# Row-centred output weights and a reordered way from cross attention into latent attention

## The chip, the cores and the metric

One core of one Trainium2 chip. The metric is the device time of one execution in microseconds (us), the median over runs; lower is better. Times of single instructions come from the profile of one execution.

## What is computed

One transformer layer over 256 rows of 512 channels. It has three parts, and each adds to the residual stream `x`: cross attention onto a context of 4096 rows (16 heads of 32), latent attention (MLA, 16 heads), and a mixture of experts. The change lies at the end of the first part and the beginning of the second:

```python
# cross attention, its end
ctx = softmax(q @ k.T / sqrt(32) + mask) @ v      # 16 heads
delta = rs * (ctx @ Wo.T + bo)                    # rs: residual scale, 0 to 0.3
mu, var = delta.mean(-1), delta.var(-1)
x = x + (delta - mu) / sqrt(var + 1e-5) * ln_gamma + ln_beta
# latent attention, its beginning
h = layernorm(x)
cq  = rms_norm(h @ w_qa.T, q_a_ln_w)              # 384 latents
ckv = h @ w_kva.T                                 # 128 latents and 64 rotary
q, kv = cq @ w_qb.T, rms_norm(ckv[:128]) @ w_kvb.T
x = x + causal_attention(q, kv, rotary) @ w_o.T
```

## The kernel before

TensorE is fed with float16 pairs: a float32 value times a scale is split into a high and a low half, by ScalarE (the high half) and then VectorE (the rest), and three products stand for one. All matmuls are issued by one helper, at L1184, so the rows below carry that line for nearly all of them.

**Cross attention** runs over 8 blocks of 512 context rows (`x_block`). A block has 8 steps `i`, the code's pairs of score tiles. In step `i` TensorE computes the scores of that step, then weighs the values with the probabilities of the step before (`weigh`), and in blocks 0 to 6 projects one of 8 units of keys or values of the next block into the one bank `pP` (`project`, which waits until ScalarE has emptied that bank of the unit before). ScalarE in each step first empties the bank (`evac`, L472 and L473 for keys) and then takes the exponents of two tiles (L540); VectorE clips them (L867) and adds them up (L879). The program of every engine is a fixed list, so whatever stands behind a wait on an engine waits too. Block 7 has no projection: there the chain from scores to exponents to the next scores sets the pace, and small work is put into its steps: on ScalarE the bias `bo` in float16 (L555, L556, step 0) and the latent weights' high halves (L558, steps 0 to 3); on VectorE the scales (`prep_scales`, L807 to L811, step 0), `x + beta` (`prep_rows`, L817, step 1), the low halves (L892, steps 2 and 3), and in steps 4 and 6 the sums of the probabilities (L897) and their reciprocals (L899), which TensorE spreads over the rows of each head in the next step.

The output weights `woT` (1 MB) lie in the place of a context buffer. SyncE's list issues their load at L349, behind the wait of block 6 for its first exponent and the load of a mask (L290):

```python
            x_block(NBLK - 2, 0, load=False)     # wait exp_done(16 * 6 + 1), load_mask(7)
            sp.wait_ge(s["ctx_lo"], 4 * (NBLK - 1))
            sp.dma_start(woT, a["woT"]).then_inc(s["wo_in"], 16)
```

In the kernel before the first to wait for `wo_in` is TensorE, in step 6 of block 7.

**The end of cross attention.** After the last `weigh`, VectorE takes the last sums and a reciprocal per 128 rows (L910, L913); TensorE spreads it by a matmul (`spread_den`), ScalarE copies it out (L574), VectorE multiplies (L851) and adds the value bias (L855), and TensorE multiplies with `woT` (`out_rows`). Then, per half `t` of the rows: mean and variance (L924, L925), the scaled variance (L926), a power by GpSimd (L448), the residual row (L930), the mean taken off (L933), four transposes (L1386), the high halves on ScalarE (L578), the squares (L580) and the low halves on VectorE (L938).

**Into latent attention.** `latents(t, low)` are the first projections, `turn_latents` (L1405) transposes their normed result, and `first_q` and `first_kv` project the queries, keys and values of head pair 0. ScalarE and VectorE then split them: rotary queries (L994, L626, L999), queries (L621, L1003), keys (L630, L1008), values (L635); then the scores of the pair start. `residual(t)` puts `x1_sb` times a scale into the banks of the output by a float32 matmul with `ident_s`, in pair 0. The output of each pair is added in these banks, first in pair 1 (`out_product`).

Of the kernel before, what the change touches and what calls it, by code (L numbers as in the profile page):

```python
# [61 lines left out]
def build(nc, a, out):  # L62
# [4 lines left out]
    with ctx:  # L67
# [34 lines left out]
        rs2 = sb("rs2", [128, 1])  # L102
# [7 lines left out]
        ident_s = sb("ident_s", [128, 128])  # L110
# [19 lines left out]
        def take(n, dt=f32):  # L130
# [133 lines left out]
            den_read rows_done den_ready denb_done rden_ready ctxn_ready delta_done  # L264
# [132 lines left out]
        def _(pool):  # L397
# [14 lines left out]
            pool.memset(ident_s[:, :], 0.0).then_inc(s["pch"], 1)  # L412
            pool.memset(onerow[:, :], 0.0).then_inc(s["pch"], 1)
            pool.memset(bo16, 0.0).then_inc(s["pch"], 1)
            chain[0] = 9
# [6 lines left out]
            for r in (0, 32):  # L422
# [17 lines left out]
                                    pattern=[[-1, 128]], channel_multiplier=1))  # L440
            link(pool.affine_select(out=ident_s[:, :], in_=ident_s[:, :], compare_op=ALU.not_equal, fill=SH * SW, base=0,
# [16 lines left out]
        def _(act):  # L458
# [63 lines left out]
            def x_block(b, p, proj=True, split=True, last=False):  # L522
                first = isinstance(b, int) and b == 0
                for i in range(PAIRS_X):
# [23 lines left out]
                    if b == NBLK - 2 and i == HC:  # L548
                        split_q(0, 0)
                        split_kv(0, 0)  # L550
                    if last and i < HC:
                        if i == 0:
                            act.wait_ge(s["const_ready"], 1)
                            act.wait_ge(s["row_in"], 64)
                            act.activation(bo16[0:1, :], bo_b[0:1, :], ACT.Copy, scale=SW)  # L555
                            act.activation(bo_t[32:33, :], bo_b[32:33, :], ACT.Copy, scale=SW).then_inc(s["bo_hi"], 1)  # L556
                            act.wait_ge(s["lat_in"], 16)
# [14 lines left out]
            for t in range(TT):  # L572
                act.wait_ge(s["denb_done"], t + 3)
                act.activation(rden[:, 3, 128 * t:128 * t + 128], pS[:, t, 0:128], ACT.Copy).then_inc(s["rden_ready"], 1)  # L574
# [71 lines left out]
            hi_latents(1)  # L646
            rope_hi(0, 0)
            mla_evac_q(0, 0, 2)
            mla_evac_k(0, 0)
# [6 lines left out]
            with act.Fori(0, PAIRS - 5, 2) as m:  # L656
                mla_pair(m, 0)
                mla_pair(m + 1, 1)
# [76 lines left out]
        def _(dve):  # L735
# [66 lines left out]
            def prep_scales():  # L802
# [5 lines left out]
                dve.tensor_tensor(rs2[:, :], rs[:, :], rs[:, :], ALU.mult)  # L808
                dve.tensor_scalar(gam_b[:, :], gam_b[:, :], rs[:, 0:1], None, ALU.mult)
                dve.wait_ge(s["bo_hi"], 1)  # L810
# [36 lines left out]
            def context(gs, cols, k):  # L847

                dve.wait_ge(s["rden_ready"], k)
                for g in gs:  # L850
                    last = dve.tensor_tensor(ctxn[:, g, cols], pO[:, g // 2, T * (g % 2):T * (g % 2) + T][:, cols],  # L851
# [330 lines left out]
        def _(pe):  # L1182
# [353 lines left out]
            def mla_pair(m, p, proj=True, before=True):  # L1536
# [10 lines left out]
                if not before:  # L1547
                    residual(0)
# [213 lines left out]
```

## Time and profile before

| | |
|---|---|
| median of 3 runs | 729.77 us (729.39 to 730.04) |
| the profiled execution | 731.32 us, its span 729.6 us |
| mean granted clock of TensorE | 0.998 |
| TensorE matmuls | 710.9 us busy, 97% |
| VectorE | 611.0 us, 84% |
| ScalarE | 435.0 us, 60% |
| GpSimd | 11.3 us, 2% |

In the span, cross attention takes until about 322 us, latent attention until about 434 us, the experts the rest. PE is TensorE's matmul part, PEld its weight loads, DVE is VectorE, ACT is ScalarE, POOL is GpSimd, SP is SyncE. The span runs from the first to the last instruction. A row of the timeline has the start, the time, the engine, the line, the operation, what it writes and reads, how many were merged, and in brackets how long the engine was idle before it and for what.

### The profile page before, as it was taken

The numbers are of one execution on the slowest core, as the hardware profiler recorded it, in microseconds if no ns is written. First come the engines' busy times: TensorE is split into PE (matmuls) and PEld (weight loads), VectorE is DVE, ScalarE is ACT, GpSimd is POOL, SyncE is SP. The second block draws the span as 40 slices with busy tenths as digits, with TensorE's granted clock in tenths as the row PEclk, the third lists the DMA queues.
The fourth block names the chain that finished last, engine by engine and source line by source line (L and its number), as shares of the span: only waits on it lengthen the run. The fifth ranks groups of instructions, "written<-read, shape, count | busy, mean of one in ns | idle before, by whom it ended". The sixth has DMA issues, their size and how long they took to land.

```text
span 729.6 us, 16489 instructions
## 1 busy us (share of the span) xinstructions
PE 710.9 (97%) x6716; PEld 441.3 (60%) x6716; DVE 611.0 (84%) x942; ACT 435.0 (60%) x597; POOL 11.3 (2%) x36
## 2 busy tenths in 40 slices
PE   8999999999999999888999989999999999999998
PEld 3544444444444444445777758777777777777775
DVE  4778999999999998776888986788888888888885
ACT  4677777777777787834668844444444444444442
POOL 3000000000000000001000000000000000000000
PEclk9999999999999999999999999999999999999999
DMA  8560101010100010014242512577777777777770
GB/s 316 176 264 1 60 2 60 1 60 2 59 3 1 12 49 1 4 47 174 77 134 92 191 44 64 175 240 238 224 243 228 234 242 245 217 242 237 227 243 33
DMA packets 29864, 94.17 MB, mean 129 GB/s; under 512 B 5824, under 2 KB 15088, under 8 KB 28400
## 3 DMA queue, kind: packets, MB, share of 16 engines
q1 hardware_dynamic: 28944, 92.31, 38.6%
q10 hardware_dynamic: 864, 1.07, 0.5%
q8 instruction: 41, 0.67, 0.4%
q14 instruction: 15, 0.12, 0.1%
HBM read 92.76 MB, written 0.57 MB: 128 GB/s over the span
## 4 chain that ended last, share of the span: by engine, by line
PE 90%; DVE 3%; ACT 3%; DMA 2%; issue 1%; SPq 0%; POOL 0%; ACTq 0%; DVEq 0%
PE pS L1184 39%; PE pP L1184 29%; PE pO L1184 13%; PE pD L1184 9%; DMA arena<-in_wkT 1%; DMA mask_i<-in_mask 1%; ACT arena L540 1%; PE pO L1552 1%; DVE arena L781 0%; DVE arena L899 0%; DVE xn L1102 0%; ACT arena L593 0%; SPq L312 0%; ACT arena L578 0%; PE pS L1386 0%
## 5 line engine op out<-in xcount | busy, mean ns | idle before, releaser
L1184 PE MATMUL pS<-arena 128*128 128x256 f16 (+3 forms) x2185 | 254.2, 273 | 1.9 <-ACT arena L578 0.8
L1184 PEld LDWEIGHTS pS<-arena 128*128 128x128 f16 (+1 forms) x2185 | 213.5, 101 | 46.2 <-issue 2.1
L1184 PE MATMUL pP<-arena 128*128 128x512 f16 x980 | 239.4, 382 | 0.6 <-ACT arena L460 0.6
L1184 PEld LDWEIGHTS pP<-arena 128*128 128x128 f16 x980 | 91.9, 99 | 124.5 <-issue 12.2
L540 ACT ACTIVATE arena<-pS,mblk 128x1024 f32<-128x1024 f32 x128 | 147.3, 1205 | 8.8 <-PE pS L1184 8.8
L1013 DVE SCALAR_TENSOR_TENSOR arena<-arena 128x1536 f16<-128x1536 f32 x72 | 126.1, 1752 | 0.8 <-ACT arena L654 0.8
L694 ACT ACTIVATE arena<-pS 128x256 f32<-128x256 f32 x72 | 27.6, 383 | 154.2 <-PE pS L1184 154.2
L1184 PE MATMUL pO<-arena 128*32 128x256 f32 (+7 forms) x1370 | 108.6, 359 | 1.9 <-DVE arena L1008 1.9
L654 ACT ACTIVATE arena<-arena 128x1536 f16<-128x1536 f32 x72 | 106.4, 1477 | 1.0 <-PE pP L1184 1.0
L867 DVE TENSOR_SCALAR arena<-arena 128x1024 f32<-128x1024 f32 x128 | 87.1, 691 | 17.6 <-ACT arena L540 14.8
L1184 PE MATMUL pD<-arena 128*128 128x512 f16 x288 | 77.9, 379 | 0.0
L1184 PEld LDWEIGHTS pO<-arena 128*32 128x32 f32 (+3 forms) x1370 | 48.8, 107 | 38.2 <-issue 17.4
L1146 DVE TENSOR_TENSOR arena<-pS,arena 128x256 f32<-128x256 f32 x72 | 30.6, 425 | 36.0 <-ACT arena L694 36.0
L1184 PE MATMUL pS<-work,arena 32*128 32x256 f16 x1536 | 53.4, 269 | 4.0 <-ACT arena L540 4.0
L1184 PEld LDWEIGHTS pS<-work,arena 32*128 32x128 f16 x1536 | 33.7, 93 | 33.5 <-issue 24.5
L1184 PEld LDWEIGHTS pD<-arena 128*128 128x128 f16 x288 | 28.2, 98 | 17.3 <-DVE arena L1158 0.2
L472 ACT ACTIVATE arena<-pP,xb 128x512 f16<-128x512 f32 x29 | 19.9, 687 | 30.9 <-PE pP L1184 30.9
L1154 DVE TENSOR_TENSOR arena<-arena 128x256 f32<-128x256 f32 x68 | 28.9, 426 | 7.7 <-DVE arena L1146 1.1
L879 DVE TENSOR_TENSOR x_sb<-x_sb,arena 128x1024 f32<-128x1024 f32 x26 | 31.8, 1222 | 1.7 <-DVE x_sb L879 0.5
L879 DVE TENSOR_TENSOR xn<-xn,arena 128x1024 f32<-128x1024 f32 x26 | 31.8, 1222 | 1.7 <-DVE xn L879 0.5
L879 DVE TENSOR_TENSOR xT<-xT,arena 128x1024 f32<-128x1024 f32 x26 | 31.8, 1222 | 1.4
L879 DVE TENSOR_TENSOR arena<-arena 128x1024 f32<-128x1024 f32 x26 | 31.8, 1222 | 1.4
(252 smaller groups left out, 493.5 us busy)
## 6 DMA issues: line engine op xcount, KB each, us to landing
arena<-in_units SPq DMA_DIRECT2D x72, 768.0 KB, 4.9
arena<-w_scratch SPq DMA_DIRECT2D x136, 64.0 KB, 2.7
arena<-in_ctxT SPq DMA_DIRECT2D x7, 1024.0 KB, 4.9
mw_in<-in_mla_in SPq DMA_DIRECT2D x8, 832.0 KB, 6.7
mw_out<-in_mla_out SPq DMA_DIRECT2D x8, 512.0 KB, 3.7
wlatT<-in_wlatT SPq DMA_DIRECT2D x1, 1280.0 KB, 10.6
arena<-in_ctxT ACTq DMA_DIRECT2D x4, 256.0 KB, 6.5
arena<-in_wkT SPq DMA_DIRECT2D x4, 256.0 KB, 5.6
```

What stands on the lines that cost most here:

```text
L472: act.activation(kh[:, p, n], bank, ACT.Identity, bias=xb[:, 1, n:n + 1], scale=1.0 / SW)
L540: act.activation(probs[:, tile], step_scores(st), ACT.Exp, bias=mblk[:, p, 1, tile:tile + 1], scale=mblk[:, p, 0, tile:tile + 1])\
L654: act.activation(uwh[:, slot], uw32[:, slot], ACT.Copy, scale=SW).then_inc(s["unit_hi"], 1)
L694: act.activation(sg[:, buf], pS[:, bank, 0:T], ACT.Silu, scale=1.0 / (SA * SW)).then_inc(s["silu_ready"], 1)
L867: dve.tensor_scalar(probs[:, t], probs[:, t], LO, HI, ALU.max, ALU.min).then_inc(s["clip_done"], 1)
L879: dve.tensor_tensor(acc, acc, probs[:, t], ALU.add).then_inc(s["sum_done"], 1)
L1013: dve.scalar_tensor_tensor(uwl[:, slot], uw32[:, slot], SW, uwh[:, slot], ALU.mult, ALU.subtract).then_inc(s["unit_lo"], 1)
L1146: dve.tensor_tensor(m1[:, buf], pS[:, bank, T:2 * T], sg[:, slot], ALU.mult).then_inc(s["m1_ready"], 1)
L1154: dve.tensor_tensor(m2[:, buf], m1[:, buf], weight, ALU.mult).then_inc(s["m2_ready"], 1)
L1184: return pe.matmul(o, lhsT, rhs, start=start, stop=stop, **kw)
L1552: last = pe.transpose(pO[:, j, 128 * i:128 * i + 128], pm[:, j, 128 * i:128 * i + 128], ident[:, :])
```

## The change

- **Centred weights.** The mean over the output channels is taken off `woT` and `bo`, so that `delta` has a mean of zero. ScalarE sums the four chunks of `woT` with an in-place copy in block 6, steps 0, 5, 6 and 7; VectorE makes means and subtracts in block 7, step 0. The bias in float16 moves to step 1 of block 7 and waits for the centred weights, `prep_rows` moves from step 1 to step 4, ahead of the sums there.
- **Variance.** `bn_stats` and `bn_aggr` are replaced by a square with an accumulator on ScalarE.
- **Last sums.** Head group 3 is summed with a matrix of ones into columns 256 to 511 of `pD`, so that every row of a head holds the sum and nothing has to be spread. VectorE multiplies, ScalarE adds the value bias; group 3 comes ahead of group 2.
- **TensorE filled.** Two and three matmuls of zeros (`keep_warm`) around the transposes of the first rows.
- **First projections.** The keys come ahead of the second half's queries, the values last; the engines behind them follow in an order of their own.
- **Residual.** Two float16 matmuls of zeros clear the banks and ScalarE writes the scaled residual there after pair 0. ScalarE's loop over the pairs has its first two written out.

Indentation is cut, and context left out:

```diff
@@ -99,7 +99,10 @@
-rs2 = sb("rs2", [128, 1])
+rsn = sb("rsn", [128, 1])
+dsq = sb("dsq", [128, TT])
+wo_sum = sb("wo_sum", [128, HC + 1])
+wo_mean = sb("wo_mean", [128, HC + 1])
@@ -107,7 +110,6 @@
-ident_s = sb("ident_s", [128, 128])
@@ -409,10 +411,9 @@
-    pool.memset(ident_s[:, :], 0.0).then_inc(s["pch"], 1)
...
-    chain[0] = 9
+    chain[0] = 8
@@ -437,8 +438,6 @@
-                            pattern=[[-1, 128]], channel_multiplier=1))
-    link(pool.affine_select(out=ident_s[:, :], in_=ident_s[:, :], compare_op=ALU.not_equal, fill=SH * SW, base=0,
@@ -548,12 +547,20 @@
+            if b == NBLK - 2 and i in (0, 5, 6, 7):
+                g = (0, 5, 6, 7).index(i)
+                if g == 0:
+                    act.wait_ge(s["wo_in"], 16)
+                    act.wait_ge(s["row_in"], 64)
+                act.activation(woT[:, g, :], woT[:, g, :], ACT.Copy, accum_out=wo_sum[:, g:g + 1])\
+                   .then_inc(s["wo_sums"], 1)
             if last and i < HC:
-                if i == 0:
+                if i == 1:
+                    act.wait_ge(s["wo_ready"], HC + 1)
...
-                    act.wait_ge(s["row_in"], 64)
...
+                if i == 0:
@@ -569,9 +576,24 @@
-    for t in range(TT):
-        act.wait_ge(s["denb_done"], t + 3)
-        act.activation(rden[:, 3, 128 * t:128 * t + 128], pS[:, t, 0:128], ACT.Copy).then_inc(s["rden_ready"], 1)
+    def add_bias(k, g, t):
+        cols = slice(128 * t, 128 * t + 128)
+        act.wait_ge(s["ctx_mul"], k)
+        act.activation(ctxn[:, g, cols], ctxn[:, g, cols], ACT.Identity, bias=xb[:, 2, g:g + 1])\
+           .then_inc(s["ctxa_ready"], 1)
+    def squares(t):
+        act.wait_ge(s["delta_done"], t + 1)
+        act.activation(scrap[:, t], d_ps[t], ACT.Square, scale=rsn[:, 0:1], accum_out=dsq[:, t:t + 1])\
+           .then_inc(s["dsq_ready"], 1)
+    add_bias(1, 3, 0)
+    add_bias(2, 2, 0)
+    squares(0)
+    add_bias(3, 3, 1)
+    add_bias(4, 2, 1)
+    squares(1)
@@ -644,16 +666,25 @@
+    mla_evac_k(0, 0, 1)
...
-    mla_evac_q(0, 0, 2)
-    mla_evac_k(0, 0)
+    mla_evac_q(0, 0, 3)
...
-    with act.Fori(0, PAIRS - 5, 2) as m:
+    def seed(t):
+        act.wait_ge(s["seed_zero"], t + 1)
+        act.activation((pD, pP)[t][:, :], x1_sb[:, t, :], ACT.Copy, scale=SH * SW).then_inc(s["seeded"], 1)
+    mla_pair(0, 0)
+    for t in range(TT):
+        seed(t)
+    mla_pair(1, 1)
+    with act.Fori(2, PAIRS - 5, 2) as m:
@@ -805,8 +836,22 @@
-        dve.tensor_tensor(rs2[:, :], rs[:, :], rs[:, :], ALU.mult)
+        dve.tensor_scalar(rsn[:, :], rs[:, :], float(HID) ** -0.5, None, ALU.mult)
...
+    def centre_bias():
+        link(dve.reduce_sum(wo_sum[:, HC:HC + 1], bo_b[:, :], AX.X))
+        dve.wait_ge(s["wo_sums"], HC)
+        link(dve.tensor_scalar(wo_mean[:, :], wo_sum[:, :], 1.0 / HID, None, ALU.mult))
+        dve.tensor_scalar(bo_b[:, :], bo_b[:, :], wo_mean[:, HC:HC + 1], None, ALU.subtract).then_inc(s["wo_ready"], 1)
+    def centre_weights(g):
+        dve.tensor_scalar(woT[:, g, :], woT[:, g, :], wo_mean[:, g:g + 1], None, ALU.subtract).then_inc(s["wo_ready"], 1)
+    def low_bias():
@@ -844,15 +889,14 @@
-    def context(gs, cols, k):
-        dve.wait_ge(s["rden_ready"], k)
+    def context(gs):
+        dve.wait_ge(s["rden_ready"], 1)
         for g in gs:
-            last = dve.tensor_tensor(ctxn[:, g, cols], pO[:, g // 2, T * (g % 2):T * (g % 2) + T][:, cols],
-                                     rden[:, g, cols], ALU.mult)
+            last = dve.tensor_tensor(ctxn[:, g, :], pO[:, 0, T * g:T * g + T], rden[:, g, :], ALU.mult)
...
         for g in gs:
-            last = dve.tensor_scalar(ctxn[:, g, cols], ctxn[:, g, cols], xb[:, 2, g:g + 1], None, ALU.add)
+            last = dve.tensor_scalar(ctxn[:, g, :], ctxn[:, g, :], xb[:, 2, g:g + 1], None, ALU.add)
@@ -884,8 +928,15 @@
-            if last and i < 2:
-                (prep_scales, prep_rows)[i]()
+            if last and i == 0:
+                centre_bias()
+                for g in range(HC):
+                    centre_weights(g)
+            if last and i == 1:
+                prep_scales()
+                low_bias()
+            if last and i == 4:
+                prep_rows()
             if last and i in (2, 3):
@@ -898,7 +949,7 @@
             if last and i == 5:
-                context((0, 1), slice(0, T), 1)
+                context((0, 1))
@@ -906,26 +957,30 @@
-    dve.wait_ge(s["rows_done"], 1)
-    link(dve.tensor_scalar(den, pD[:, 0:T], 1e-30, None, ALU.max))
     def last_den(t):
...
-        dve.reciprocal(rd[:, 0, cols], den[:, cols]).then_inc(s["den_ready"], 1)
+        link(dve.tensor_scalar(den[:, cols], pD[:, T + 128 * t:T + 128 * t + 128], 1e-30, None, ALU.max))
+        link(dve.reciprocal(rden[:, 3, cols], den[:, cols]))
+    def weighted(g, t):
+        cols = slice(128 * t, 128 * t + 128)
+        dve.tensor_tensor(ctxn[:, g, cols], pO[:, 1, T * (g % 2):T * (g % 2) + T][:, cols], rden[:, g, cols],
+                          ALU.mult).then_inc(s["ctx_mul"], 1)
+    dve.wait_ge(s["rows_done"], 1)
...
-    context((2,), slice(0, T), 2)
-    context((3,), slice(0, 128), 3)
+    weighted(3, 0)
+    dve.wait_ge(s["rden_ready"], 2)
+    weighted(2, 0)
...
-    context((3,), slice(128, T), 4)
+    weighted(3, 1)
+    weighted(2, 1)
     for t in range(TT):
-        dve.wait_ge(s["delta_done"], t + 1)
-        link(dve.bn_stats(bn[:, t, :], d_ps[t]))
-        link(dve.bn_aggr(mv[:, t, :], bn[:, t, :]))
-        dve.tensor_scalar(var[:, t:t + 1], mv[:, t, 1:2], rs2[:, 0:1], 1e-5, ALU.mult, ALU.add)\
-           .then_inc(s["var_ready"], 1)
-        link(dve.scalar_tensor_tensor(work[:, t, :], d_ps[t], mv[:, t, 0:1], gam_b[:, :], ALU.subtract, ALU.mult))
+        dve.wait_ge(s["dsq_ready"], t + 1)
+        dve.tensor_scalar(var[:, t:t + 1], dsq[:, t:t + 1], 1e-5, None, ALU.add).then_inc(s["var_ready"], 1)
+        link(dve.tensor_tensor(work[:, t, :], d_ps[t], gam_b[:, :], ALU.mult))
@@ -1051,10 +1106,10 @@
-    rope_mul(0, 0, 1)
+    lo_k(0, 0, 1)
+    rope_mul(0, 0, 2)
...
-    lo_q(0, 0)
-    lo_k(0, 0)
+    lo_q(0, 0, 2)
@@ -1274,6 +1329,14 @@
+    def sum_cols(g):
+        return slice(T, 2 * T) if g == HC - 1 else slice(0, T)
+    def sum_weights(g):
+        return ones[:, 0:32] if g == HC - 1 else onecol[:, g, :]
@@ -1284,7 +1347,7 @@
                 for j in range(4):
-                    last = mm(pD[32 * j:32 * j + 32, 0:T], onecol[:, g, :], probs[:, tile, j, :], False,
+                    last = mm(pD[32 * j:32 * j + 32, sum_cols(g)], sum_weights(g), probs[:, tile, j, :], False,
@@ -1308,17 +1371,17 @@
         for j in range(4):
-            last = mm(pD[32 * j:32 * j + 32, 0:T], onecol[:, g, :], psums[g][:, j, :], False, False,
+            last = mm(pD[32 * j:32 * j + 32, sum_cols(g)], sum_weights(g), psums[g][:, j, :], False, False,
...
-    def out_rows(t, gs):
+    def out_rows(t, gs, end=True):
...
         for g in gs:
-            done = mm(d_ps[t], ctxn[:, g, 128 * t:128 * t + 128], woT[:, g, :], False, g == HC - 1)
+            done = mm(d_ps[t], ctxn[:, g, 128 * t:128 * t + 128], woT[:, g, :], False, end and g == 2)
@@ -1345,6 +1408,7 @@
+                pe.wait_ge(s["wo_ready"], HC + 1)
@@ -1359,26 +1423,23 @@
-    def spread_den(t):
-        pe.wait_ge(s["den_ready"], t + 3)
-        mm(pS[:, t, 0:128], selrow[:, 3, :], rd[:, 0, 128 * t:128 * t + 128], True, True).then_inc(s["denb_done"], 1)
+    def keep_warm(n, o):
+        for _ in range(n):
+            mm(o, zero16[:, 0:128], zero16[:, :], True, True)
...
-    spread_den(0)
-    pe.wait_ge(s["ctxn_ready"], 2)
-    out_rows(0, (2,))
-    pe.wait_ge(s["ctxn_ready"], 3)
-    out_rows(0, (3,)).then_inc(s["delta_done"], 1)
-    spread_den(1)
-    out_rows(1, (1, 2))
-    pe.wait_ge(s["ctxn_ready"], 4)
-    out_rows(1, (3,)).then_inc(s["delta_done"], 1)
-    def keep_warm(n, o):
-        for _ in range(n):
-            mm(o, zero16[:, 0:128], zero16[:, :], True, True)
+    pe.wait_ge(s["ctxa_ready"], 1)
+    out_rows(0, (3,), False)
+    pe.wait_ge(s["ctxa_ready"], 2)
+    out_rows(0, (2,)).then_inc(s["delta_done"], 1)
+    out_rows(1, (1,), False)
+    pe.wait_ge(s["ctxa_ready"], 3)
+    out_rows(1, (3,), False)
+    pe.wait_ge(s["ctxa_ready"], 4)
+    out_rows(1, (2,)).then_inc(s["delta_done"], 1)
+    keep_warm(2, pD[:, :])
@@ -1413,13 +1474,13 @@
+    keep_warm(3, pD[:, :])
...
-    pe.wait_ge(s["ctxn_ready"], TT + 2)
@@ -1439,15 +1500,21 @@
-    def first_kv(t):
+    def first_k(t):
...
-        for j in range(2):
-            at = QC * QW + 128 * j
-            for k, (w, x) in enumerate(PARTS):
-                last = mm(pS[:, 2, T * j + 128 * t:T * j + 128 * t + 128], w[:, at:at + 128], x[:, QC, cols], k == 0, k == 2)
+        for k, (w, x) in enumerate(PARTS):
+            pe.wait_ge(s["lat_lo" if k == 2 else "lat_hi"], t + 1)
+            for j in range(2):
+                at = QC * QW + 128 * j
+                last = mm(pS[:, 2, T * j + 128 * t:T * j + 128 * t + 128], w[:, at:at + 128], x[:, QC, cols],
+                          j == 0 and k == 0, j == 1 and k == 2, skip_group_check=True)
         if t == TT - 1:
...
+    def first_v(t):
+        cols = slice(128 * t, 128 * t + 128)
         for k, (w, x) in enumerate(PARTS):
@@ -1488,6 +1555,7 @@
+            pe.wait_ge(s["seeded"], TT)
         if t == 0 or last:
@@ -1496,9 +1564,10 @@
-    def residual(t):
-        mm((pD, pP)[t][:, :], ident_s[:, :], x1_sb[:, t, :], True, False, skip_group_check=True)
+    def clear(t):
+        mm((pD, pP)[t][:, :], zero16[:, 0:128], zero16[:, :], True, False, skip_group_check=True)\
+            .then_inc(s["seed_zero"], 1)
@@ -1545,7 +1614,8 @@
         if not before:
-            residual(0)
+            clear(0)
+            clear(1)
@@ -1553,8 +1623,6 @@
-        else:
-            residual(1)
@@ -1568,10 +1636,12 @@
-    first_kv(0)
+    first_k(0)
+    first_v(0)
+    first_k(1)
...
-    first_kv(1)
+    first_v(1)
...
```

## Rows read from the trace of the kernel before

**Rows 1.** Page, part 1: busy us, share of the span, instructions.

```profile
PE 710.9 (97%) x6716; PEld 441.3 (60%) x6716; DVE 611.0 (84%) x942; ACT 435.0 (60%) x597; POOL 11.3 (2%) x36
```

**Rows 2.** Timeline, block 6, steps 0 and 1.

```profile
253.15 0.59 SPq L349 DMA_DIRECT2D arena<-in_woT  x1
...
255.07 0.69 ACT L472 ACTIVATE arena<-pP,xb 128x512 f16<-128x512 f32 x1 [1.38 <-PE pP L1184]
255.66 0.68 ACT L473 ACTIVATE arena<-pP,xb 128x512 f32<-128x512 f32 x1
...
256.73 2.76 PE L1184 MATMUL pP<-arena 128*128 128x512 f16 x12
```

**Rows 3.** DMA issues, 250 to 262 us: KB each, median us from issue to landing.

```profile
arena<-in_woT SPq DMA_DIRECT2D x1, 1024.0 KB, 5.4
```

**Rows 4.** Timeline, from the last sums to the first latents.

```profile
318.07 0.95 DVE L913 RECIPROCAL arena<-arena 128x128 f32<-128x128 f32 x1
...
320.16 0.29 DVE L851 TENSOR_TENSOR arena<-pO,arena 128x128 f32<-128x128 f32 x1 [0.47 <-ACT arena L574]
...
322.01 2.74 PE L1184 MATMUL pP<-arena 128*128 128x512 f32 x6
...
323.99 0.21 DVE L926 TENSOR_SCALAR var<-mv,rs 128x1 f32<-128x1 f32 x1
...
324.95 0.75 DVE L930 SCALAR_TENSOR_TENSOR x_sb<-work,rstd,x_sb 128x512 f32<-128x512 f32 x1
...
327.67 0.62 ACT L580 ACTIVATE arena<-xn 128x512 f32<-128x512 f32 x1
...
328.19 0.19 ACT L580 ACTIVATION_READ_ACCUMULATOR arena<-xn 128x1 f32 x1
```

**Rows 5.** Timeline, block 7, steps 0 to 4.

```profile
290.58 0.62 ACT L555 ACTIVATE arena<-bo_b 1x512 f16<-1x512 f32 x1
...
291.21 0.63 ACT L556 ACTIVATE arena<-bo_b 1x512 f16<-1x512 f32 x1
...
291.59 0.48 DVE L809 TENSOR_SCALAR gam_b<-gam_b,rs 128x512 f32<-128x512 f32 x1
291.87 0.74 ACT L558 ACTIVATE arena<-wlatT 128x640 f16<-128x640 f32 x1
...
295.43 1.29 DVE L817 TENSOR_TENSOR x_sb<-x_sb,bet_b 128x512 f32<-128x512 f32 x2
...
295.74 2.30 ACT L540 ACTIVATE arena<-pS,mblk 128x1024 f32<-128x1024 f32 x2 [0.32 <-PE pS L1184]
...
305.16 0.42 DVE L897 TENSOR_SCALAR arena<-pD 128x256 f32<-128x256 f32 x1
```

**Rows 6.** Chain that ended last, 286 to 352 us: start us, us, what.

```profile
305.62 1.76 DVE arena L899
...
307.51 1.10 PE pP L1184 x4
...
326.48 0.67 PE pS L1386 x4
...
331.66 0.45 PE pS L1386 x4
...
336.88 0.67 PE pD L1405 x4
```

**Rows 7.** Busy time by stretch: us, PE, PEld, DVE, ACT, POOL, PEclk, DMA, GB/s.

```profile
327.50:328.00 0.50, 0.09 (x2) 0.12 (x3) 0.50 (x1) 0.50 (x2) 0.42 (x1) 0.50 0.97 406
...
330.50:331.00 0.50, 0.50 (x3) 0.17 (x2) 0.00 (x0) 0.00 (x0) 0.50 (x1) 0.67 1.02 430
```

**Rows 8.** Timeline, pair 0's splits, and ScalarE's first exponents of pair 1.

```profile
342.20 0.69 DVE L994 SCALAR_TENSOR_TENSOR arena<-pS,arena 128x512 f32<-128x512 f32 x1 [0.43 <-PE pS L1184]
...
344.79 0.68 DVE L1008 SCALAR_TENSOR_TENSOR arena<-pS,arena 128x512 f16<-128x512 f32 x1
...
361.04 0.37 ACT L593 ACTIVATE arena<-pO,arena 128x128 f32<-128x128 f32 x1 [2.65 <-DVE arena L1029]
```

More of the change, by code:

```diff
@@ L263, in build @@
             scores_done exp_done clip_done pv_done sum_done dsum_done
-            den_read rows_done den_ready denb_done rden_ready ctxn_ready delta_done
+            den_read rows_done ctx_mul ctxa_ready dsq_ready wo_sums wo_ready seed_zero seeded den_ready denb_done rden_ready ctxn_ready delta_done
             wl_hi wl_lo bo_hi bo_ready xsq_ready xl1_ready lat_mm kpe_mm kpn_ready kpe_hi kpe_tr ssq_ready lvar_ready lrstd_ready latn_ready lat_tr lat_hi lat_lo mq_hi mq_lo mkv_hi mkv_lo kpe_ready
@@ L1361, in _ @@
             weigh(NBLK - 1, 1, PAIRS_X - 1, True)
-            def spread_den(t):
-                pe.wait_ge(s["den_ready"], t + 3)
-                mm(pS[:, t, 0:128], selrow[:, 3, :], rd[:, 0, 128 * t:128 * t + 128], True, True).then_inc(s["denb_done"], 1)
-            pe.wait_ge(s["rden_ready"], 2)
-            out_rows(1, (0,))
-            spread_den(0)
-            pe.wait_ge(s["ctxn_ready"], 2)
-            out_rows(0, (2,))
-            pe.wait_ge(s["ctxn_ready"], 3)
-            out_rows(0, (3,)).then_inc(s["delta_done"], 1)
-            spread_den(1)
-            out_rows(1, (1, 2))
-            pe.wait_ge(s["ctxn_ready"], 4)
-            out_rows(1, (3,)).then_inc(s["delta_done"], 1)
             def keep_warm(n, o):
@@ L1381, in keep_warm @@
                     mm(o, zero16[:, 0:128], zero16[:, :], True, True)
+            pe.wait_ge(s["rden_ready"], 2)
+            out_rows(1, (0,))
+            pe.wait_ge(s["ctxa_ready"], 1)
[8 more added lines that the diff above has]
+            keep_warm(2, pD[:, :])
             def turn_rows(t):
```

## The prediction

> **What bounds the kernel now.** I read the page first: TensorE's matmuls are busy for 97% of the span, and no other engine comes near [rows 1]. Where TensorE never waits, a microsecond of waiting put into it is a microsecond of time. The windows and the chain of waits then show three kinds of stretches. In blocks 0 to 6 TensorE's own work is the path; ScalarE empties the one projection bank just ahead of need. In block 7 and on the way into latent attention the path runs from engine to engine. In latent attention's pairs and in the experts TensorE leads again. The change touches the first kind once (a sum of weights in block 6) and the second kind in most of its parts.
>
> The numbers below are of the profiled execution, 731.32 us with 1.72 outside its span; the median shown is 729.77, 1.55 less, and I carry the same difference over.
>
> **1. The sum of the first weight chunk, block 6, step 0.** ScalarE now waits there for `wo_in`. SyncE's list isn't changed: the load is issued at 253.15 [rows 2], since it stands behind the first exponent of that block, and takes 5.4 to land [rows 3], so it lands at 258.55. Before, ScalarE was idle 1.38 and began to empty the bank at 255.07, was done at 256.34, and TensorE took up the next unit at 256.73 [rows 2]. Queued behind the new wait on ScalarE are the copy with its accumulator (0.71 from start to the read's end, as L580 has it [rows 4]), the bank's emptying (1.27) and the exponents of step 1 (2.30, as in [rows 5]). So the bank is free at 258.55 + 0.71 + 1.27 = 260.5, and TensorE, which has only scores and one weighing to do before, stands idle from 256.73: **+3.8**. The exponents follow by 262.8, before the projection of 2.76 is over (263.3), and add nothing. Nothing gives it back, for TensorE has no gap in this block. Ends: 3.0 if the landing is seen some 0.8 earlier, 4.4 if later. The sums of steps 5 to 7 (0.71 each) fit into ScalarE's idle time, which was 1.38 in the step shown and is larger where a value unit is emptied by one instruction: 0; without that cover 0.7 each.
>
> **2. The clock after that idle time.** No row shows an idle time of 3.8 in this stage. The nearest: TensorE stands idle from 324.75 [rows 4] to its transposes at 326.48 [rows 6], and then runs at half of its 2.4 GHz from before 327.5 until within 330.5 to 331 [rows 7]. The latents' first part, eight matmuls of 512 columns and eight of 128, lay in this stretch and took 3.9, from 327.8, when ScalarE is done with their high halves (it begins L580 at 327.67), to 331.66 [rows 4, 6]. At 12 matmuls of 512 in 2.76 [rows 2] eight take 1.8 and the small ones 0.45: 2.3. So a fall cost 1.5 there. An idle time twice as long should bring one more surely: **+1.5**. Ends: 0, and 2.8 if the fall lasts on after the bank is freed.
>
> **3. Block 7, steps 0 and 1.** VectorE has, after its clips at about 291.3, a sum over 512 (0.69, as L994 [rows 8]), two small links (0.25) and five subtractions of 0.48 that overlap by 0.08 each [rows 5], as L809: all centred at 294.3. ScalarE, whose exponents of step 1 end before (from 291.6 to 293.9), waits for that, then has the two bias copies (290.58 to 291.84, 1.26) and the weights' split (0.74) ahead of the exponents of step 2: these start at 296.2 instead of 295.74 [rows 5]: **+0.45**. Ends: 0 and 0.9. VectorE's clips of step 1 end at 295.5 as before. The weights' own sums are there since block 6.
>
> **4. `prep_rows` in step 4.** In step 1 its 1.29 [rows 5] ran in VectorE's idle time. In step 4 it stands ahead of the sums (305.16) and their reciprocal (305.62 to 307.38), for which TensorE waits at 307.51, with the scores of step 6 queued behind [rows 5, 6]. There is no cover: **+1.35** with one link. Ends: 0.9 and 1.4.
>
> **5. From the last sums to the transposes.** The maximum is taken over 128 columns instead of 256, so the reciprocal starts about 0.13 sooner than 318.07 and ends at 318.9. The product (0.29, L851) ends at 319.2, ScalarE's addition (0.37, L593 [rows 8]) at 319.65. TensorE, done with the second half's first rows at 319.6, needs 1.2 for the first of two products (0.2 to load weights, 0.43 for each of its two instructions, from 2.74 for six) and 0.86 for the second: the delta stands at 321.7. The square from the bank with two pointers takes about 0.8 (0.71 for L580): 322.5. From there on as before, where the scaled variance at 323.99 led to the residual at 324.95 and to transposes at 326.48 [rows 4, 6]: 322.55 + 0.96 + 1.53 = 325.05. But TensorE is late itself: ScalarE does the addition for the second half only after the square, at 322.85, so its products end at 324.9 and the two filling matmuls at 325.35. The transposes begin there, 1.13 sooner: **-1.15**. Ends: -0.6 and -1.6. What is late next is TensorE, and at the second half nothing: its row is ready at 328.2, before TensorE asks.
>
> Of the additions' place the rows say: VectorE takes 0.29 for such a step, ScalarE 0.37 [rows 4, 8], so ScalarE costs 0.08 once, while VectorE is spared two steps ahead of its second reciprocal. By the Trainium skill, "ScalarE: Activation LUTs", Rules for kernel authors, additions belong on VectorE and not on ScalarE, which speaks against this step of the change; the trace agrees on the single instruction, and by the rule this part would be -1.25 with them left on VectorE, where the sum above has -1.15.
>
> **6. The first latents at full clock.** With TensorE idle for no more than 0.6 at a time in that stretch, the fall of part 2's rows does not happen: **-1.5**. Ends: 0 and -1.7. The first part then ends at 329.0 instead of 331.66, and the chain to the transposed latents (331.66 to 336.88 [rows 6]), all of it at full clock, moves as it is.
>
> **7. First projections.** Before, the rotary product began 342.20, and VectorE's last of four splits ended 345.47 [rows 8]. Now VectorE starts with the keys' low half, which needs ScalarE's high half first (0.6), and has one pause, for the rotary high half, as before: 342.0 + 0.6 + 3.25 = 345.85. **+0.4**. Ends: -0.3 and +0.6.
>
> **8. The residual.** Both float32 matmuls ran while TensorE waited for VectorE and ScalarE, so 0 is gained; if one wasn't covered, 0.9. ScalarE's two writes (0.6 each) stand ahead of the weights' split for pair 2, and ScalarE was idle 2.65 before its exponents of pair 1 [rows 8]: 0; without that cover 1.2. The constants' two instructions fewer on GpSimd lie in its 98% idle time: 0.
>
> Sum: 3.8 + 1.5 + 0.45 + 1.35 - 1.15 - 1.5 + 0.4 = **+4.85**: 736.2 for a profiled execution, **734.6** for the median.
>
> **Rivals.**
> *The clock doesn't fall in block 6* (0.22). The array is busy right up to the wait, which speaks for it; the shorter idle time at 324.75 that was enough speaks against. +3.35: 733.1.
> *`prep_rows` stays covered* (0.06): if TensorE's wait for the reciprocal had slack. The 307.38 and 307.51 above say no. +3.5: 733.3.
> *ScalarE's wait is absorbed* (0.08), the one that ends on the other side. It is one mechanism: the weights are there before ScalarE comes to its wait in block 6. It decides at 254.4, the latest landing at which a copy of 0.71 is done by 255.1; then parts 1 and 2 are gone and -0.45 is left: 729.3, no change. For it speaks only that the load is asked for before ScalarE arrives; against it the 5.4, as this leaves 1.2.
> *ScalarE's residual writes delay pair 1* (0.04): +1.2 more, 735.8.
> *The tail gains nothing, for the clock falls there too* (0.05): +6.35, 736.1.
>
> **How the numbers follow.** The forecast has 0.55. Its own range, with the ends of its terms, goes from 733 to 737. 0.2% (about what a measurement of this kernel can tell from no change) is 1.46 us. The range reaches down to the case without a fall with its lower ends, 731.6, and up to 737.4; the absorbed wait lies outside. Slower by over 0.2%: the forecast and all rivals but one, less what their lower ends leave, 0.89. Within: 0.08, of which most is the absorbed wait. Faster: 0.03, that case with a tail at its best end.
>
> **What would show it.** Part 1: a row of idle time on ScalarE of about 3.8 or more before the copy of `woT`, released by the DMA, and on TensorE one of about 3.8 in front of the projection of that step. Part 2: a granted clock of 0.50 right behind it. Part 4: `prep_rows` between the clips of step 4 and the sums, the pair of scores in step 6 starting 1.3 later against step 5. Part 5: 7.4 instead of 8.4 from the last reciprocal to the first transposes. Part 6: granted clock 1.00 throughout the latents. Part 7: 0.4 more from the transposed latents to the first scores. The prediction is wrong if ScalarE doesn't wait for `wo_in`, or if TensorE's work in block 6 is no longer than before.

## The result and the profile after

The changed kernel takes 736.68 us in the median of 4 runs (735.51 to 737.45), the kernel before 729.90 in 4 (729.39 to 730.89): 1.009 times as long, 95% interval 1.007 to 1.0109. The profiled execution took 737.32 with a span of 735.6, 6.0 more than before's.

The page's part 1 after: TensorE has 1.7 us more of busy time and VectorE 0.6, against 6 us more of span. ScalarE has 6.0 more, in 16 instructions more, but is busy for 60% only. So most of the 6 us is waiting and clock [rows 1].

```profile
PE 712.6 (97%) x6715; PEld 441.4 (60%) x6715; DVE 611.6 (83%) x944; ACT 441.0 (60%) x613; POOL 10.9 (1%) x34
```

**Block 6**, the timeline of the changed kernel, which answers to [rows 2] (the load is now L351, the chunk's sum L555, the bank's emptying L471 and L472):

```profile
254.51 0.59 SPq L351 DMA_DIRECT2D arena<-in_woT  x1
...
259.56 0.63 ACT L555 ACTIVATE arena<-arena 128x512 f32<-128x512 f32 x1 [4.51 <-DMA arena<-in_woT]
260.09 0.19 ACT L555 ACTIVATION_READ_ACCUMULATOR arena<-arena 128x1 f32 x1
260.18 0.67 ACT L471 ACTIVATE arena<-pP,xb 128x512 f16<-128x512 f32 x1
260.75 0.68 ACT L472 ACTIVATE arena<-pP,xb 128x512 f32<-128x512 f32 x1
...
261.49 4.45 PE L1239 MATMUL pP<-arena 128*128 128x512 f16 x12 [3.33 <-ACT arena L472]
```

ScalarE is idle for 4.51 and the load releases it. TensorE is idle for 3.33 behind it, and its 12 matmuls then take 4.45, where they took 2.76 [rows 2]. The windows of the same kernel say why, with the columns of [rows 7]:

```profile
261.00:262.00 1.00, 0.52 (x2) 0.21 (x3) 0.54 (x1) 1.00 (x2) 0.00 (x0) 0.90 0.00 0
262.00:263.00 1.00, 1.00 (x4) 0.40 (x3) 0.60 (x2) 1.00 (x2) 0.00 (x0) 0.50 0.00 0
```

**From block 7 on**, the chain of the changed kernel, which answers to [rows 6]: `prep_rows` (L862) now stands in it, ahead of the sums' reciprocal (L950).

```profile
312.15 1.30 DVE x_sb L862 x2
313.45 0.02 issue
313.47 0.43 DVE arena L948
313.91 0.02 issue
313.93 1.76 DVE arena L950
...
315.83 1.10 PE pP L1239 x4
...
333.14 0.43 PE pD L1239 x2
333.58 0.44 PE pS L1447 x4
...
337.05 0.45 PE pS L1447 x4
...
342.27 0.67 PE pD L1466 x4
...
351.70 2.37 PE pO L1239 x36
```

The two filling matmuls stand in it too (333.14), directly before the transposes, as forecast. Stage by stage, from the starts of the same instructions in both traces (in the chains from the spread of the sums on). The two stretches left out between the first lines are unchanged (216.93 in both, and 31.31 against 31.32), so the three later sums of weights in block 6 and the centring cost nothing there:

| stretch | before | after | difference | forecast |
|---|---|---|---|---|
| start to block 0's first projection by steps | 38.04 | 39.39 | +1.35 | 0 |
| block 6, scores of step 1 to those of step 2 | 4.46 | 9.55 | +5.09 | +5.3 |
| block 7, scores of step 1 to the spread of the first sums | 16.77 | 18.64 | +1.87 | +1.8 |
| to the first transposes | 18.97 | 17.75 | -1.22 | -1.15 |
| to the second transposes | 5.18 | 3.47 | -1.71 | -1.5 |
| to the transposed latents | 5.22 | 5.22 | 0.00 | 0 |
| to the first scores of pair 0 | 8.85 | 9.43 | +0.58 | +0.4 |
| to the end | 383.87 | 383.90 | +0.03 | 0 |

The first line is in code that the change leaves alone. There the query projection's last part took longer, 5.01 for the same 29 matmuls instead of 3.34. The chain before, the chain after, and a window after, which has half clock:

```profile
22.98 3.34 PE pS L1184 x29
```

```profile
22.67 5.01 PE pS L1239 x29
```

```profile
23.00:24.00 1.00, 1.00 (x7) 0.69 (x6) 1.00 (x3) 0.00 (x0) 0.00 (x0) 0.50 0.06 10
```

Of the nine profiles of kernels with the change and this stretch as it is, two have the fall there (this one and that of the sum in step 2), so it comes in some executions only. None of the three profiles of the kernel before and its variants has it; these are too few to say that the kernel before never has it.

### The profile page after: what moved, and what is told of

Same layout as the page of the kernel before. It is cut to its first block, busy times and chain, and to the rows that moved or that the text cites. A ratio compares the mean times of both kernels' runs of the same rounds, so it can differ in the third digit from the quotient of the medians.

```text
span 735.6 us, 16479 instructions
## 1 busy us (share of the span) xinstructions
PE 712.6 (97%) x6715; PEld 441.4 (60%) x6715; DVE 611.6 (83%) x944; ACT 441.0 (60%) x613; POOL 10.9 (1%) x34
## 3 DMA queue, kind: packets, MB, share of 16 engines
q10 hardware_dynamic: 864, 1.07, 0.5%
## 4 chain that ended last, share of the span: by engine, by line
PE 89%; DVE 3%; DMA 3%; ACT 3%; issue 1%; SPq 0%; POOL 0%; ACTq 0%; DVEq 0%
PE pS L1239 38%; PE pP L1239 29%; PE pO L1239 12%; PE pD L1239 9%; DMA arena<-in_wkT 1%; DMA mask_i<-in_mask 1%; ACT arena L539 1%; DMA arena<-in_woT 1%; PE pO L1622 1%; DVE arena L812 0%; DVE arena L950 0%; ACT arena L615 0%; DVE arena L851 0%; DVE xn L1157 0%; DVE x_sb L862 0%
## 5 line engine op out<-in xcount | busy, mean ns | idle before, releaser
L471 ACT ACTIVATE arena<-pP,xb 128x512 f16<-128x512 f32 x29 | 19.9, 686 | 30.8 <-PE pP L1239 30.8
```

The source lines that it names most:

```text
L471: act.activation(kh[:, p, n], bank, ACT.Identity, bias=xb[:, 1, n:n + 1], scale=1.0 / SW)
```

## The experiments

Each ran on a chip beside runs of the kernel before. Of 53 such runs 26 had a mean granted clock of 1.00 (medians of the three sets 729.93, 730.08 and 730.12) and 27 one of 0.998 (731.59, 731.80, 731.66): one fall of the clock is worth about 1.6 us of the time. So each result is read twice: by its ratio to before, and by its profile in the stretches of the table. The ratio on record is not the quotient of the two medians and differs from it by up to 0.001.

The mean clock of a run tells how many falls it had: the profiles with one fall have 0.998 or 0.997, those with two 0.995, and the one with 0.993 has two, of which one lasted twice as long. Where the falls were, only the one profile of each kernel shows.

The changed kernel itself was not run again beside these runs. Where a median is set against its 736.68, that number comes from the first set, whose kernel before had 729.90; beside the runs below the kernel before has 730.57, 730.38 and 731.42. Differences of medians under about 1 us should not be read from this.

**The wait for the weights.**

```diff
-            if b == NBLK - 2 and i in (0, 5, 6, 7):
+            if b == NBLK - 2 and i in (2, 5, 6, 7):
```

> The changed kernel, with the first chunk of the output weights summed in step 2 of block 6 instead of step 0. If the wait for the weights' load is what holds block 6 (3.4 us of TensorE idle in the changed kernel's profile) and the half clock behind it the rest (1.7), both go: 5.1 less than the changed kernel, so about -0.5 against the kernel before when no other fall of the clock differs, and a granted clock of 1.00 through block 6. The rival, that the copy with its accumulator is too long for a step in which keys are emptied as well, expects TensorE to stand idle in step 3 by some tenths to 0.7, and at least 0.7 more time. The second rival, that the load's traffic itself slows the engines, expects no more than half of the 5.1.

Measured: 732.36, ratio to before 1.0016 (1.0005 to 1.0028), 4.3 below the changed kernel. The block 6 stretch is back at 4.46, with full clock there. ScalarE's copy fits: the next keys are emptied 0.40 after it.

```profile
264.56 0.64 ACT L555 ACTIVATE arena<-arena 128x512 f32<-128x512 f32 x1
265.08 0.21 ACT L555 ACTIVATION_READ_ACCUMULATOR arena<-arena 128x1 f32 x1
...
265.69 0.69 ACT L471 ACTIVATE arena<-pP,xb 128x512 f16<-128x512 f32 x1 [0.40 <-PE pP L1239]
```

So in block 6 the wait is the cause, as expected, and both rivals fall. The total was not -0.5 but +1.8: I had counted a gain of 1.5 from the clock in the latents that exists only against a run of before in which it falls. Where both have a mean clock of 1.00 the medians are 730.92 and 729.93, +1.0; the table's lines without that gain give 1.87 - 1.22 - 0.30 + 0.58 = +0.9 (0.30 is what the latents gain against a full clock, see the wait alone below). The profiled run (732.3 of span) also has two falls elsewhere: one at the start (+1.69), and one that was new, in pair 0's first scores (+1.46), behind an idle time of 2.37 of TensorE.

```diff
+    sp.wait_ge(s["ctx_lo"], 4 * (NBLK - 1))
+    sp.dma_start(woT, a["woT"]).then_inc(s["wo_in"], 16)
     x_block(NBLK - 2, 0, load=False)
-    sp.wait_ge(s["ctx_lo"], 4 * (NBLK - 1))
-    sp.dma_start(woT, a["woT"]).then_inc(s["wo_in"], 16)
```

> The changed kernel, with the load of the output weights issued before block 6's wait for its first exponent instead of behind it; the first sum stays in step 0. If only the landing is late, this gives the same 5.1 as the sum in step 2 (within 0.3), and ScalarE shows no idle time released by the load. If the copy's place in step 0 matters (0.71 in an idle time of 1.38), TensorE starts its projection in step 1 later than before by a tenth or more. If it is the load's traffic that slows block 6, it is as slow as the changed kernel.

Measured: 732.29, ratio 1.0025 (1.0012 to 1.0037). The sum stays in step 0, but the weights are there, and the block 6 stretch is 4.47:

```profile
253.25 0.62 ACT L554 ACTIVATE arena<-arena 128x512 f32<-128x512 f32 x1
253.78 0.19 ACT L554 ACTIVATION_READ_ACCUMULATOR arena<-arena 128x1 f32 x1
254.74 0.69 ACT L470 ACTIVATE arena<-pP,xb 128x512 f16<-128x512 f32 x1 [0.77 <-PE pP L1238]
```

Only the landing was late. Two different edits that take the wait away give the same stretch. This profile has one fall, in pair 0's first scores (+0.98).

```diff
+    if b == NBLK - 2 and i == 1:
+        for _ in range(15):
+            mm(pD[:, :], zero16[:, 0:128], zero16[:, :], False, False, skip_group_check=True)
     if proj:
         project(b + 1, 1 - p, i)
```

> The changed kernel, with 15 matmuls of zeros (0.22 each, 3.2 in all) added onto the bank of the sums in step 1 of block 6, where TensorE waits. The wait stays at about 3.4. If the half clock behind the wait comes from the idle time, the clock stays at 1.00 and the kernel is 1.7 faster than the changed one. If the clock falls anyway, or the matmuls outlast the wait, nothing is gained or some tenths are lost.

Measured: 735.07, ratio 1.0062 (1.0047 to 1.0077), 1.6 below the changed kernel. The stretch is +3.31 instead of +5.09, so in the profile the fall is worth 1.78 and the wait 3.3. TensorE's timeline, and the clock:

```profile
256.52 3.41 PE L1239 MATMUL pD<-zero 128*128 128x512 f16 x15
259.83 2.76 PE L1239 MATMUL pP<-arena 128*128 128x512 f16 x12
```

```profile
260.00:261.00 1.00, 1.00 (x6) 0.47 (x5) 0.60 (x2) 1.00 (x2) 0.00 (x0) 1.00 0.07 16
```

That the zeros held the clock is likely but rests on few runs. All six profiles with the wait unfilled have the fall. By the mean clock 3 of the 33 runs with it unfilled have no fall at all, and 2 of the 6 filled ones.

The wait was then put into the kernel before, alone (TensorE also waits for the copy, in step 6 of block 7, where it is long done):

```diff
+    if b == NBLK - 2 and i == 0:
+        act.wait_ge(s["wo_in"], 16)
+        act.activation(woT[:, 0, :], woT[:, 0, :], ACT.Copy, accum_out=wo_sum[:, 0:1])\
+           .then_inc(s["wo_sums"], 1)
```

> The kernel before, with one thing of the change: in step 0 of block 6 ScalarE waits for the output weights' load and copies their first chunk in place with an accumulator. If this wait by itself makes block 6's loss, TensorE's step 1 is 3.3 to 3.6 longer plus 1.7 where the clock falls behind the idle time (it fell in most profiles of the changed kernel, not in all): 5.1 in the profile, 4 to 5 in the median, +0.6%. If it needs the other parts of the change, nothing or less than 1.

Measured: 735.05, ratio 1.0057 (1.004 to 1.0074). In the profile the block 6 stretch is +5.02:

```profile
258.22 0.63 ACT L554 ACTIVATE arena<-arena 128x512 f32<-128x512 f32 x1 [4.54 <-DMA arena<-in_woT]
...
260.15 4.35 PE L1189 MATMUL pP<-arena 128*128 128x512 f16 x12 [3.36 <-ACT arena L474]
```

The one wait, without the rest of the change, is most of the slowdown: 5.0 of the profile's 6.0, and 3.6 of 6.8 by the medians. Its one run without a fall took 733.81, 3.7 more than the kernel before without one.

In this profile the latents ran at full clock (their stretch is 3.77, 1.41 less than before) although nothing was changed there. So where the falls come differs from execution to execution. The same eight matmuls behind the same idle time, in the profile of before and in this one:

```profile
327.91 1.01 PE L1184 MATMUL pS<-arena 128*128 128x128 f16 x8 [0.78 <-ACT arena L578]
```

```profile
332.93 0.61 PE L1189 MATMUL pS<-arena 128*128 128x128 f16 x8 [0.78 <-ACT arena L583]
```

**Block 7.**

```diff
-    if last and i == 4:
+    if last and i == 7:
         prep_rows()
```

> The changed kernel, with x + beta added in step 7 of block 7, where VectorE is idle for 1.34 before the last sums, instead of in step 4 ahead of the sums. By my reading the step from the exponents of step 4 to the scores of step 6 is 1.3 shorter, and the last sums are not later: 1.3 faster than the changed kernel. If TensorE had slack behind the reciprocal of step 4 (rival), nothing is gained; if the addition in step 7 sticks out ahead of the last sums, 0.1 to 0.5 of the gain is given back.

Measured: 736.50, ratio 1.0072 (1.0057 to 1.0087). The medians do not show the gain; the profile does: the block 7 stretch is +0.55 instead of +1.87, so 1.3 as forecast. The way from there to the transposes is 0.08 longer, but VectorE is idle for 0.21 between the addition and the last sums, so the addition does not stick out:

```profile
322.58 1.29 DVE L862 TENSOR_TENSOR x_sb<-x_sb,bet_b 128x512 f32<-128x512 f32 x2
324.08 0.29 DVE L962 TENSOR_SCALAR arena<-pD 128x128 f32<-128x128 f32 x1 [0.21 <-PE pD L1239]
```

All 5 of its runs had a mean clock of 0.995 or 0.993. In the profile, with 0.993, the fall in block 6 lasted twice as long (the stretch is +6.04) and pair 0's scores had one (+1.07).

```diff
-        if i == 1:
-            act.wait_ge(s["wo_ready"], HC + 1)
...
+    if last and i == 4:
+        act.wait_ge(s["wo_ready"], HC + 1)
...
     if last and i == 1:
         prep_scales()
-        low_bias()
...
     if last and i == 5:
+        low_bias()
         context((0, 1))
```

> The changed kernel, with the bias's two copies on ScalarE (and their wait for the centred weights) in step 4 of block 7 instead of step 1, and the bias's low half on VectorE in step 5. In the changed kernel the exponents of step 2 start 4.66 after those of step 1, where the chain from scores to exponents allows 3.24; so 1.4 should be gained, since in step 4 ScalarE is not what the next step waits for. If VectorE's clips of step 1, which come behind the centring, were the bound (rival), only 0.5 or less is gained.

Measured: 736.39, ratio 1.0075 (1.0061 to 1.0089); its runs had clocks of 0.995 to 0.992. In the profile the block 7 stretch is +0.48, 1.4 less than in the changed kernel. The exponents of steps 1 and 2 are 3.25 apart:

```profile
296.62 2.30 ACT L539 ACTIVATE arena<-pS,mblk 128x1024 f32<-128x1024 f32 x2 [0.32 <-PE pS L1239]
298.82 0.73 ACT L560 ACTIVATE arena<-wlatT 128x640 f16<-128x640 f32 x1
299.87 2.30 ACT L539 ACTIVATE arena<-pS,mblk 128x1024 f32<-128x1024 f32 x2 [0.32 <-PE pS L1239]
```

VectorE's clips are not the bound. 0.9 of the 1.4 were lost by the kernel before too, which had the copies in step 0: with the sums moved as well (all four below) the stretch is 0.86 shorter than before.

**The way into latent attention.** The order of the first projections and of the splits behind them was set back:

```diff
-    first_k(1)
     first_q(1, 1)
     first_q(1, 0)
+    first_k(1)
     first_v(1)
...
-    lo_k(0, 0, 1)
-    rope_mul(0, 0, 2)
+    rope_mul(0, 0, 1)
     rope_lo(0, 0)
-    lo_q(0, 0, 2)
+    lo_q(0, 0)
+    lo_k(0, 0)
```

> The changed kernel, with the second halves of the first projections and the splits behind them in the order of the kernel before (rotary queries first, keys after the queries). From the transposed latents (the transposes of the first half) to the first scores the kernel before took 8.85, the changed one 9.43. If the order is the cause, 0.6 is gained and the first split is the rotary product again. If it is something else in that stretch, the 9.43 stays.

Measured: 735.17, ratio 1.0057 (1.0037 to 1.0077). The stretch is 8.85 again, 0.58 less than in the changed kernel. Changed, and then with the old order:

```profile
347.54 0.60 ACT arena L652
348.14 0.02 issue
348.17 0.69 DVE arena L1063
348.86 0.61 DVE arena L1049
349.47 0.02 issue
349.49 0.64 ACT arena L648
```

```profile
345.87 0.70 DVE arena L1049
346.57 0.02 issue
346.59 0.64 ACT arena L648
```

The new order puts ScalarE's high half of the keys (0.60) ahead of everything; the pause for the rotary half stays.

```diff
-    keep_warm(2, pD[:, :])
...
-    keep_warm(3, pD[:, :])
```

> The changed kernel without the five matmuls of zeros on the way into latent attention. My reading is that the fall of the clock there came from TensorE's idle time of 1.7 before the transposes; in the changed kernel the idle times without the five would be about 0.3 and 1.0. If these are too short for a fall, the time stays within 0.3 of the changed kernel, and may be 0.1 to 0.2 less; if the filling is what holds the clock, it falls to 0.50 behind the transposes and 1.5 are lost.

Measured: 736.22, ratio 1.0084 (1.0066 to 1.0102). In the profile the clock stays at 1.00 in that stretch, the first transposes come 0.13 earlier, the second ones at the same time as in the changed kernel. The filling is not what held the clock in this execution. The clocks of the 6 runs (0.998 four times, 0.995, 0.993) are too few to say that it never helps.

```diff
     out_rows(1, (3,)).then_inc(s["delta_done"], 1)
...
+    keep_warm(7, pD[:, :])
...
     pe.wait_ge(s["wl_lo"], HC)
+    keep_warm(3, pD[:, :])
     latents(0, False)
```

> The kernel before, with 7 matmuls of zeros after the delta's last product and 3 behind the first transposes, in the idle times of 1.7 and 0.8. If the half clock in the first latents comes from those idle times, it stays at 1.00, and the first latents are 1.5 shorter: 1.5 faster than before (0.2%), less a tenth if the seven outlast the wait. If the clock falls anyway, no difference.

Measured: 730.03 against 730.38, ratio 0.9995 (0.9985 to 1.0005). In the profile the stretch to the second transposes is 1.49 shorter at a clock of 1.00, as expected, but the median moves by 0.35 only, and the interval includes no change. 8 of its 12 runs have a mean clock of 1.00, and 10 of the 17 beside it. Whether the filling took a fall away is not shown: in the profile of the wait alone the latents had full clock unfilled. What is shown is that the fall in the profile of before comes in some executions only, and that 4 of the 12 filled runs still have one, in a place that no profile shows.

**Together.**

> The changed kernel with all four steps set right: the first chunk summed in step 2, x + beta in step 7, the bias's copies in step 4, the old order of the first projections. From the single runs, stage by stage against the kernel before: block 6 0, block 7 -0.9, last sums to transposes -1.25, to the second transposes -1.5 only where the kernel before has its fall of the clock, first projections 0. So -2.1 with no fall in either and -3.6 against a kernel before with one; median about 2.5 below the kernel before (0.35%). If the single gains don't add up, for instance because step 4 or 5 of block 7 is now too full, it is 1 or less below it.

The diff is the sum of those of the sum in step 2, of the rows in step 7, of the late bias and of the old order. Measured: 728.97 against 731.42, ratio 0.9968 (0.9955 to 0.998), faster than both kernels. Block 6 +0.00, block 7 -0.86, from there to the second transposes -2.85 (the changed kernel: -2.93), first projections +0.05; pair 0's scores had a fall (+1.14). Its two runs without a fall took 727.41 and 727.44, 2.7 less than the kernel before without one, where -2.1 was expected.

```diff
+    if g == 0:
+        mm(pS[:, 3, :], zero16[:, 0:128], zero16[:, :], False, False, skip_group_check=True)
     pe.wait_ge(s["wq_lo"], c + 1)
...
     first_v(1)
+    keep_warm(8, pD[:, :])
```

> The kernel with all four steps set right, and matmuls of zeros in two other idle stretches of TensorE in which the clock was seen to fall: 4 between the query projection's waits at the beginning, 8 ahead of the first scores of latent attention. If the spread between its runs (1.5 to 1.7 per fall) comes from those places, all runs show a clock of 1.00 and the median is that of the kernel without them in its best runs, 0.5 to 1 below its median. If falls come elsewhere too, or the filling sticks out, the clock still varies and nothing is gained.

Measured: 727.73, ratio 0.9955 (0.9942 to 0.9968). All 5 runs have a mean clock of 1.00, and they lie within 727.44 to 727.91, where the runs without the fills reach from 727.41 to 729.95. The median is 1.24 lower, and 0.3 above the two best runs without fills. 5 of 5 runs without a fall, against 2 of 8, speaks for the fills; which of the two places did it was not tried apart. Two windows, one ahead of the first scores and one behind their start, without and with the fills:

```profile
341.00:342.00 1.00, 0.00 (x0) 0.00 (x0) 1.00 (x2) 1.00 (x3) 0.00 (x0) 1.00 0.00 0
...
344.00:345.00 1.00, 1.00 (x9) 0.43 (x4) 0.06 (x1) 0.00 (x0) 0.00 (x0) 0.50 0.00 0
```

```profile
341.00:342.00 1.00, 1.00 (x6) 0.29 (x3) 1.00 (x2) 1.00 (x3) 0.00 (x0) 1.00 0.00 0
...
344.00:345.00 1.00, 1.00 (x11) 0.90 (x10) 0.33 (x1) 0.00 (x0) 0.00 (x0) 1.00 0.00 0
```

## Why the prediction was right

The direction, the main cause and the range held: 736.68 against 734.6, within 731.6 to 737.4, though one of the four runs (737.45) lies above it. The forecast difference was +4.85, the profile's is +6.0, of which +1.35 is at the start, in code that the change leaves alone; the terms that were forecast come to +4.65. Point by point:

1. The wait: +3.8 forecast, 3.3 measured, in the row and with the clock held. The landing took 5.0 instead of the 5.4 of [rows 3] (4.9 to 5.1 in seven more profiles). The terms behind it, 0.71 and 1.27, were nearly as worked out: from the copy to TensorE's start it is 1.93.
2. The clock behind it: +1.5 forecast, 1.8 measured by filling the wait. The nearest row served well, and the rival without a fall was wrong for every profile with the wait unfilled, but not for every run: two of the six with the old order and one of the six with the wait alone had a mean clock of 1.00.
3. and 4. Block 7: +1.8 forecast, +1.87 measured. In the starts of the scores it is +0.54 up to step 3, where +0.45 was forecast, and +1.33 from step 5 to step 6, where +1.35 was. Moving the rows out of step 4 alone gives 1.3 back, as priced; the copies' later place gives 1.4, more than the 0.54 that the change added, for 0.9 were lost before.
5. To the transposes: -1.15 forecast, -1.22 measured (from the last reciprocal 7.33 instead of 8.41, where 7.4 was forecast). TensorE's products and the two fills set the end, as said. That the additions fit on ScalarE is seen in the chain, where they and the square are in turn the last. One took 0.39 there, where VectorE took 0.29 before, so the 0.37 of the forecast was a little low; the four additions were not tried on VectorE.
6. The latents' clock: -1.5 forecast, -1.71 measured, **but this is the step that was wrong in kind**. I took the fall at 327.5 [rows 7] for a property of the kernel before. It is one of some executions: half of the runs of before (26 of 53) have no fall at all. Against those the change gains 0.30 there and not 1.71, for the stretch is 3.77 at full clock in the profile of the wait alone and 3.47 in the changed kernel. The forecast even took that fall twice: the 1.55 between the profile and the median of before, which it carried over, is about one fall, and part 6 took 1.5 off again for the same one. Without part 6 it says 736.1. The rest of the 2.1 by which the measured median lies above 734.6 comes from falls that I did not count, such as the one at the start: the four runs of the changed kernel have one (735.51, 736.04) or two (737.32, 737.45).
7. First projections: +0.4 forecast, +0.58 measured, and 0.58 given back by the old order.
8. The residual: 0 forecast. ScalarE's two writes (0.61 and 0.60) stand before its first exponents of pair 1, which still wait 1.62 for VectorE; from the first scores to the end the profiles differ by 0.03.

```profile
363.72 0.61 ACT L681 ACTIVATE pD<-x_sb 128x512 f32<-128x512 f32 x1
364.24 0.60 ACT L681 ACTIVATE pP<-x_sb 128x512 f32<-128x512 f32 x1
364.76 0.63 ACT L519 ACTIVATE arena<-mw_in 128x512 f16<-128x512 f32 x1
367.00 0.37 ACT L615 ACTIVATE arena<-pO,arena 128x128 f32<-128x128 f32 x1 [1.62 <-DVE arena L1084]
```

What stays open: whether the new order raises the chance of a fall in pair 0's scores. Its idle time there is 2.37, where the old order has 1.91 to 1.95; a fall came behind both, in 4 of the 7 profiles with the new order and in 1 of the 5 with the old one and no filling there. That points to the new order, but is too few to show it.

## What to carry to other kernels

When an operand gets an earlier first reader, look up where the queue issues its load, not only whether the load was ahead of the old reader: here a good change to the tail lost five microseconds some seventy microseconds away. Work moved along a list should be priced at its new place by what waits behind it there. When a clock fall stands in the one trace that is read, ask how many of the runs have it before a gain is booked against it.

## What was not expected of the hardware

The granted clock falls to its lower level in this kernel at four places, behind idle or thinly filled stretches of TensorE: in the query projection at the start (four short waits of 0.3), behind the wait in block 6 (3.3), in the first latents (1.7 and 0.8), and in pair 0's first scores (1.9 to 2.4). Runs of one program differ by up to two falls (by the mean clock none to two with the sum in step 2, for example), and each adds 1.0 to 1.8 us. The idle time alone does not decide it: behind the same waits at the start (0.3 each), in the latents (0.78) and before pair 0's scores (2.37) one execution has a fall and another has none. The falls made most of the spread between runs of one kernel: with two of the places filled with matmuls of zeros it is 0.5 us (5 runs), without them 2.5 us (8 runs).
